# Products of B and the inputs for two of eight state groups moved from VectorE to GpSimd in a state-space layer

## The reference

```python
x_and_res = x @ W_in                          # 128 -> 2 * 256
xs = silu(conv(xc) + conv_b)                  # 256 inner channels
x_dbl = xs @ W_x                              # dt_r (64), Bm (16), Cm (16)
dt = softplus(dt_r @ W_dt + b_dt)
dA = exp(dt[..., None] * A)                   # (batch, time, 256, 16)
dBx = einsum('bld,bln->bldn', dt, Bm) * xs[..., None]
h[t] = dA[t] * h[t - 1] + dBx[t]              # the scan over time
y[t] = einsum('bdn,bn->bd', h[t], C[t]) + xs * D
out = (y * silu(res)) @ W_out
```

## Time and profile before

| | |
|---|---|
| median of 3 runs | 2748.03 us (2746.03 to 2750.99) |
| profiled execution, its own time | 2754.61 us |
| its span | 2752.4 us |
| busy share of the span | PE 87%, PEld 61%, DVE 72%, ACT 64%, POOL 54% |
| first scan to the end of the last (L1797) | 864.0 to 1167.0 us |
| first and last scan 0 of a batch | 863.95 and 1134.24 us, seven periods |

### The profile page before, as it was taken

One profiled execution on the slowest core, in us unless ns is written; L12 is line 12 of the kernel. 1 busy time (PEld: TensorE's weight loads), 2 busy tenths in 40 slices (PEclk: granted clock), 3 DMA queues, 4 the chain that ended last, 5 costly groups with the idle time before them and its releaser, 6 DMA issues.

```text
span 2752.4 us, 93948 instructions
## 1 busy us (share of the span) xinstructions
PE 2392.0 (87%) x35312; PEld 1682.1 (61%) x35340; DVE 1982.8 (72%) x3051; ACT 1770.8 (64%) x3674; POOL 1476.6 (54%) x1060
## 2 busy tenths in 40 slices
PE   7999857896475777768999999999999999999995
PEld 4777535665353334336777777777777767777774
DVE  5888644222325888877888888888888888888883
ACT  4666432333225677666877787778877788777883
POOL 2444324213212444546777777677776777777770
PEclk9999978997787999889999999999999999999998
DMA  9100004772231000001112112211211211121111
GB/s 332 44 0 0 13 22 131 224 223 72 62 108 61 1 0 0 0 16 32 31 53 60 32 30 53 50 42 30 61 38 41 58 46 30 30 69 46 30 30 32
DMA packets 143485, 153.91 MB, mean 56 GB/s; under 512 B 12272, under 2 KB 111920, under 8 KB 142256
## 3 DMA queue, kind: packets, MB, share of 16 engines
q1 hardware_dynamic: 139312, 144.53, 19.1%
q0 software_dynamic: 4096, 8.40, 1.0%
HBM read 75.29 MB, written 27.26 MB: 37 GB/s over the span
## 4 chain that ended last, share of the span: by engine, by line
PE 51%; issue 3%; PEld 1%; DVE 1%; ACT 1%; PEldq 0%; DVEq 0%; POOL 0%; POOLq 0%; ACTq 0%
PE ps L2028 12%; PE ps L2039 6%; PE ps L2126 6%; PE ps L2074 6%; PE ps L2096 5%; PE ps L2152 4%; PE ps L2063 4%; PE ps L2085 3%; PE ps L2161 3%; PE ps L2055 1%; PE ps L2141 1%; PE ps L2134 1%; ACT Y L1406 0%; DVE ss L2531 0%; PEld ps L2126 0%
## 5 line engine op out<-in xcount | busy, mean ns | idle before, releaser
L2427 POOL TENSOR_TENSOR c<-a,bq 128x1024 f32<-128x1024 f32 x192 | 454.0, 2365 | 239.9 <-DVE bq L2524 239.1
L2437 POOL TENSOR_TENSOR qn<-c,ss 128x1024 f32<-128x1024 f32 x192 | 378.0, 1969 | 28.4 <-issue 4.0
L2028 PE MATMUL ps<-wqk,xs 128*128 128x512 f32 x768 | 371.5, 607 | 11.0 <-POOL xs L2420 9.1
L2523 DVE TENSOR_TENSOR a<-ps,tab 128x512 f32<-128x512 f32 x384 | 262.8, 684 | 10.1 <-ACT sq L2234 4.8
L2524 DVE TENSOR_TENSOR bq<-ps,tab 128x512 f32<-128x512 f32 x384 | 261.1, 680 | 0.0
L2445 POOL TENSOR_TENSOR z<-z,sm 128x1024 f32<-128x1024 f32 x96 | 182.6, 1903 | 142.9 <-DVE sm L2552 142.9
L2234 ACT ACTIVATE sq<-ps 128x512 f32<-128x512 f32 x384 | 215.3, 596 | 59.9 <-PE ps L2028 59.7
L2531 DVE TENSOR_REDUCE ss<-sq 128x16 f32<-128x1024 f32 x192 | 230.5, 1217 | 31.0 <-issue 16.6
L1489 POOL TENSOR_TENSOR hC<-hs,Cs 128x1024 f32<-128x1024 f32 x64 | 150.5, 2356 | 176.9 <-ACT Cs L1641 90.4
L2028 PEld LDWEIGHTS ps<-wqk,xs 128*128 128x128 f32 x768 | 140.1, 193 | 136.1 <-issue 129.8
L2039 PEld LDWEIGHTS ps<-ident,qn 128*128 128x128 f32 x1536 | 175.8, 141 | 67.5 <-issue 47.5
(11 more groups left out here) (316 smaller groups left out, 5381.7 us busy)
## 6 DMA issues: line engine op xcount, KB each, us to landing
Vw<-Vs SPq DMA_DIRECT2D x192, 256.0 KB, 4.2
win_rows<-rows_q SPq DMA_DIRECT2D x24, 256.0 KB
outs_q<-win_out SPq DMA_DIRECT2D x24, 256.0 KB
wqk<-in_wqkv SPq DMA_DIRECT2D x6, 1024.0 KB, 5.0
leaves<-in_f_w SPq DMA_DIRECT2D x9, 576.0 KB
leaves<-in_q_w SPq DMA_DIRECT2D x1, 4608.0 KB, 18.8
leaves<-in_k_w SPq DMA_DIRECT2D x1, 4608.0 KB, 22.8
leaves<-in_v_w SPq DMA_DIRECT2D x8, 576.0 KB
```

The source lines that it names most:

```text
L2028: nc.tensor.matmul(jobs.out(n), xs[:, t * 128:(t + 1) * 128], wqk[:, (2 * y + s) * 512:(2 * y + s + 1) * 512], start=True, stop=True).then ...
L2427: nc.gpsimd.tensor_tensor(f(c), f(a), f(bq), ALU.add).then_inc(c_ready.sem, 1)
L2437: nc.gpsimd.tensor_tensor(qn[:, t, y, :, :, :].rearrange("p h s e -> p h (s e)"), c[:, y, :, :, :].rearrange("p h s e -> p h (s e)"), spre ...
L2523: nc.vector.tensor_tensor(a[:, y, :, s, :], Zs, spread(table(0, s), H1), ALU.mult)
```

## The change

For groups 3 and 6 (`SIDE`) the product of B and du is made by GpSimd instead of VectorE. ScalarE copies B of these groups from PSUM to a new SBUF tile `Bs` (`take_B`), and signals it after a drain. GpSimd multiplies it by du into a second new SBUF tile `dBs` in one instruction of 1024 columns. In GpSimd's queue the product for group 3 stands behind read_out 0, the one for group 6 behind read_out 3. In ScalarE's queue take_B 3 stands between decay 1 and decay 2, take_B 6 ahead of decay 6. The scans of groups 3 and 6 read dBs from SBUF in place of dBx in PSUM, and wait for it. GpSimd's loop is written as pairs of batches, since du has two halves.

```diff
--- before.py
+++ after.py
@@ -1424,6 +1424,8 @@
         xdbl = sb("xdbl", [DTR, T])
         dA, hs, hC = (sb(n, [128, 2, 2, 2, T]) for n in ("dA", "hs", "hC"))
         Cs = sb("Cs", [128, 2, 2 * T])
+        SIDE = {3: 0, 6: 1}
+        Bs, dBs = sb("Bs", [128, len(SIDE), 2 * T]), sb("dBs", [128, len(SIDE), 2, 2 * T])
 
         dBx = core.banks.ps[:, 0:2, :]
         S = lambda n, per, credit=0: Count(core.sem("l1a_" + n), per, credit)
@@ -1432,6 +1434,7 @@
             S(n, 1) for n in ("xdbl", "part1", "rest1", "part2", "rest2", "parts", "soft", "dt"))
         dA_ready, hs_ready, hC_ready, hC_used, yy_ready = (
             S("dA", NG), S("hs", NG, 2), S("hC", NG, 2), S("hC_used", NG - 1), S("yy", 1))
+        du_ready, Bs_ready, dB_ready = S("du", 1), S("Bs", len(SIDE)), S("dB", len(SIDE), len(SIDE))
         consts = core.sem("l1a_consts")
         FRONT, MID = range(2)
         order = ((FRONT, "mean", 2), (MID, "Y", 7), (MID, "C2", 3), (MID, "C3", 2), (FRONT, "var", 5), (MID, "C4", 4), (MID, "B4", 6),
@@ -1472,6 +1475,17 @@
                 pool.drain()
                 pool.sem_inc(consts, 1)
                 pool.sem_inc(hC_ready.sem, hC_ready.credit)
+                pool.sem_inc(dB_ready.sem, dB_ready.credit)
+
+                def input_states(b, g, du):
+
+                    i = SIDE[g]
+                    if not (type(b) is int and b == 0):
+                        pool.wait_ge(hs_ready.sem, hs_ready.at(b, g + 1, NG))
+                    pool.wait_ge(du_ready.sem, du_ready.at(b, 1))
+                    pool.wait_ge(Bs_ready.sem, Bs_ready.at(b, i + 1))
+                    nc.gpsimd.tensor_tensor(dBs[:, i, :, :].rearrange("p k (j l) -> p k j l", j=2),
+                                            spread(halves(Bs[:, i, :]), 2), spread(du[:, :, :], 2, 2), ALU.mult).then_inc(dB_ready.sem, 1)
 
                 def read_out(b, g):
 
@@ -1488,11 +1502,17 @@
                     pool.wait_ge(hs_ready.sem, hs_ready.at(b, g + 1))
                     nc.gpsimd.tensor_tensor(four(hC), four(hs), spread(Cs[:, s, :], 2), ALU.mult).then_inc(hC_ready.sem, 1)
 
-                for g in range(NG):
-                    read_out(0, g)
-                with pool.Fori(1, NB) as b:
+                def batch(b, y):
                     for g in range(NG):
                         read_out(b, g)
+                        if g in (0, 3):
+                            input_states(b, g + 3, du2[:, y, :, :])
+
+                batch(0, 0)
+                with pool.Fori(0, (NB - 2) // 2) as pair:
+                    batch(pair * 2 + 1, 1)
+                    batch(pair * 2 + 2, 0)
+                batch(NB - 1, 1)
 
             @block.tensor
             def _(pe):
@@ -1640,6 +1660,13 @@
                     act.wait_ge(*jobs.filled(made(b, f"C{g}"), f"C{g}"))
                     nc.scalar.activation(Cs[:, g % 2, :], jobs.out(f"C{g}"), ACT.Copy).then_inc(jobs.sem_drained(f"C{g}"), 1)
 
+                def take_B(b, g):
+                    act.wait_ge(dB_ready.sem, dB_ready.at(b, SIDE[g] + 1, len(SIDE)))
+                    act.wait_ge(*jobs.filled(made(b, f"B{g}"), f"B{g}"))
+                    nc.scalar.activation(Bs[:, SIDE[g], :], jobs.out(f"B{g}"), ACT.Copy).then_inc(jobs.sem_drained(f"B{g}"), 1)
+                    act.drain()
+                    act.sem_inc(Bs_ready.sem, 1)
+
                 def square_centered(it):
                     act.wait_ge(*jobs.taken(it, "mean"))
                     nc.scalar.activation(lsq[:, :], cent[:, :], ACT.Square).then_inc(squared.sem, 1)
@@ -1698,6 +1725,7 @@
                     new, old = dt2[:, y, :, :], dt2[:, 1 - y, :, :]
                     if mid:
                         decay(b, 1, old)
+                        take_B(b, 3)
                         decay(b, 2, old)
                         take_C(b, 0)
                         decay(b, 3, old)
@@ -1719,6 +1747,7 @@
                         gates(it, xs, sres)
                         take_dbl(it, parts)
                     if mid:
+                        take_B(b, 6)
                         decay(b, 6, old)
                         take_C(b, 5)
                     if front:
@@ -1780,7 +1809,7 @@
 
                 def steps_by_input(dt, du, xs):
                     dve.drain()
-                    nc.vector.tensor_tensor(flat(du), flat(dt), flat(xs), ALU.mult)
+                    nc.vector.tensor_tensor(flat(du), flat(dt), flat(xs), ALU.mult).then_inc(du_ready.sem, 1)
 
                 def input_states(b, g, du):
                     dve.drain()
@@ -1793,8 +1822,12 @@
                     dve.drain()
                     dve.wait_ge(hC_ready.sem, hC_ready.at(b, g + 1, 2))
                     dve.wait_ge(dA_ready.sem, dA_ready.at(b, g + 1))
+                    states = flat(dBx)
+                    if g in SIDE:
+                        states = flat(dBs[:, SIDE[g], :, :])
+                        dve.wait_ge(dB_ready.sem, dB_ready.at(b, SIDE[g] + 1))
                     one_row = lambda t: t[:, g % 2, :, :, :].rearrange("p k j l -> p (k j l)")
-                    nc.vector.tensor_tensor_scan(one_row(hs), one_row(dA), flat(dBx), 0.0, ALU.mult, ALU.add).then_inc(hs_ready.sem, 1)
+                    nc.vector.tensor_tensor_scan(one_row(hs), one_row(dA), states, 0.0, ALU.mult, ALU.add).then_inc(hs_ready.sem, 1)
 
                 def gated(it, xs, sres):
                     dve.wait_ge(*jobs.filled(it, "Y"))
@@ -1820,7 +1853,6 @@
                         center(it)
                     if mid:
                         scan(b, 2)
-                        input_states(b, 3, old_du)
                     if front:
                         by_root(it)
                     if mid:
@@ -1831,8 +1863,6 @@
                         scan(b, 5)
                     if front:
                         first_rest(it, parts)
-                    if mid:
-                        input_states(b, 6, old_du)
                     if front:
                         second_rest(it, parts)
                     if mid:
```

## The result

| | median us | runs |
|---|---|---|
| before | 2749.51 (2745.44 to 2754.06) | 6 |
| changed | 2796.38 (2791.18 to 2805.01) | 6 |

The ratio is 1.0181, with a 95% interval from 1.0165 to 1.0198: the change makes the kernel 46.9 us slower. The forecast was 2804 us with a range from 2781 to 2818.

What follows compares the result with a forecast made beforehand. VectorE was taken to set the stage's pace, with little room in a ring of waits through hC. Seven periods at 7.5 us plus 3 for the last batch gave 55.5 us, hence 2804 us on the median of 2748.0; range 2781 to 2818.

Steps and rivals of the forecast that it cites:

- The main step: State-space stage: removing 2.9 us per batch from VectorE makes it slower through queue waits and blocked scans; slower 0.95.
- Scan 1 to 2: Copy of B 3 on ScalarE makes C 0 1.1 us late, so OUT and add_out wait: VectorE 0.5 us late.
- Scan 2 to 3: dBs 3 ahead of hC 1 delays the copies of C, root_variance and by_root before scan 3: 1.8 us more.
- The blocked scans: Scans 3 and 6, both inputs in SBUF, stand still until GpSimd's hC 2 or hC 5 ends: 0.7 and 2.0 us.
- du held by hC 6: Behind scan 6, hC 6 starts with the product dt and then holds up du: 0.4 us.
- Scan 5 to 6: Copy of B 6 and dBs 6 delay hC 4, which scan 6 needs: 7.3 us where it was 5.02, 2.3 more.
- The sum: Terms give 7.7 us per period, settling at 7.4, taken as 7.5; 55.5 us in all with the last batch.
- scan 0 to 1: Up to the next scan 1 the order is as before and TensorE's Y keeps its distance: nothing.
- The last batch: No front part; hC 1 late by 0.5, scan 4 held by hC 2, scan 6 delayed and held: about 3 us.
- Without blocking: Rival, 14%: queue delay only, scans not stopped by GpSimd; 4.7 us per period, 35 in all, 2783 us.
- Faster: Rival, 3%: both dBs lie in GpSimd's idle time, so VectorE loses 2.9 us per batch: 2725 us.
- the dearer case: Rival, 8%: GpSimd product costs 2.75 us or more, or scans also hold hC: 12 us more, 2816 us.

Runs made afterwards that it cites:

- The run with the pairs kept: Changed kernel, with VectorE still making the removed pairs of products on dBx, where nobody reads them: 2800.06 us, 54.1 more than before.
- the last two runs: Two single edits of the changed kernel: copy of B 3 behind that of C 0, 2778.24 us; dBs 3 ahead of hC 0 on GpSimd, 2791.04 us.
- the scan from SBUF alone: Kernel before, with VectorE writing the products of groups 3 and 6 to SBUF, from where scans 3 and 6 read them: 2761.29 us.
- the run with the copies: Changed kernel with group 6 alone moved, and ScalarE copying the finished dBs to dBx in PSUM for scan 6: 2761.47 us, 14.4 more than before.
- the run with both products moved: Changed kernel, both GpSimd products moved to idle places of its queue, copies of B and making of B 6 reordered: 2763.91 us, 16.8 more than before.

## Why the prediction was right, point by point

**The main step held.** VectorE is the busiest engine of the stage, work was taken from it, and the stage got slower, since each new instruction stands in an in-order queue ahead of one that VectorE waits for, and since two scans were blocked. The run with the pairs kept shows that the saved time lies in waits. The terms below are against the mean of the seven periods before, if nothing else is said.

**Scan 1 to 2** was put at 0.5 us and is 1.9. The place and the order were right: the copy of B 3 at 992.35, C 0 at 994.74, OUT at 995.37, add_out at 997.42. What was mis-sized is TensorE on that path. It had waited 3.29 us for hC 7 before 988.23. The windows around it (PE busy in the third column, PEclk third from the end):

```profile
982.00:986.00 4.00, 2.86 (x8) 0.88 (x6) 3.50 (x2) 0.76 (x2) 0.84 (x2) 1.00 0.00 0
986.00:988.00 2.00, 0.00 (x0) 0.00 (x0) 1.73 (x3) 0.00 (x0) 2.00 (x1) 1.00 0.00 0
988.00:991.30 3.30, 3.07 (x5) 1.09 (x6) 3.14 (x3) 2.18 (x5) 0.17 (x1) 0.62 0.00 0
991.30:995.00 3.70, 1.02 (x5) 0.40 (x3) 3.19 (x5) 2.46 (x6) 0.00 (x0) 0.87 0.00 0
995.00:998.00 3.00, 2.63 (x8) 1.87 (x9) 1.16 (x2) 2.02 (x5) 2.52 (x2) 0.61 0.00 0
```

Right behind the idle stretch the granted clock is 0.62 on average, at half (1.2 GHz) for most of the window and at full (2.4 GHz) for the rest, and in OUT's window 0.61. The four matmuls of over_states 7 take 3.24 us, C 0 with B 3 1.06 and OUT 1.84, where C 0 with B 3 took 0.60 and OUT 1.13. The prediction took these durations at the clock of before. 0.5 for B 3 and 0.7 for OUT make 1.2 of the missing 1.4 us. It is so in every batch: the seven OUT that add_out waited for took 1.84 to 2.08 us at a clock of 0.50 to 0.57, while before five of seven took 1.13 at 1.00. With group 3 alone, two periods had OUT at 1.00 and in 1.13 us, and there scan 1 to 2 took 5.39 and 5.25 us, 0.7 more than the same periods before (4.67 and 4.53); its other periods took 6.3 to 6.8.

**Scan 2 to 3** was put at 1.8 and is 0.7. With scan 2 already late, less of the delay of hC 1 is left to wait for; the sum of both terms was put at 2.3 and is 2.6. That the sum came out near is in part luck. The prediction gave too much of it to dBs 3 and too little to C 0, as the last two runs show.

**The blocked scans.** 0.7 for scan 3 and 2.0 for scan 6 were worked out from one collision of du with hC. Measured are 2.98 - 2.29 = 0.69 and 4.34 - 2.29 = 2.05. The end of the blocked scan is 2.15 us behind the end of the GpSimd product; 2.14 was forecast. Two runs show the cause: the scan from SBUF alone brings 15.4 us, and one PSUM input takes 13.2 away again. du held by hC 6 was put at 0.4 and takes 1.21 to 1.39 us in place of 0.69. Together, scan 6 to 7 is 2.4 us longer than in six of the seven periods before, as forecast, and 2.0 above their mean, for the first of them had a collision of its own (8.36 us). The rule of the Trainium skill (SBUF — State Buffer, Who interferes with whom), that a VectorE instruction with two SBUF inputs contends with a GpSimd instruction that reads SBUF, holds for the scan too; the traces agree (scan 6 beside hC 5: 2.29 us with one input in PSUM in the run with the copies, 4.43 with both in SBUF in the run with group 6 alone).

**Scan 5 to 6** was put at 2.3 and is 1.7 against the mean of before. Scan 6 waits for hC 4 behind dBs 6, as said. The length was forecast at 7.3 us and is 7.03; against the batch shown in the rows the term is 2.0.

**The sum.** The period was forecast at 45 us and is 45.14. The total was 8.6 us too high (55.5 against 46.9). Per period 7.5 us were forecast and 6.5 are measured, 1.9 + 0.7 + 0.7 + 1.7 + 2.0 + 0.1 - 0.6 by the stretches. Most of this difference is the last multiplication: 7.5 us were counted against the period of rows 1, 37.86 us, one of the shortest, while the mean of the seven before is 38.61. The long ones of before held waits for Y and a blocked du, which the new waits swallow. 7 x 0.75 = 5.3 us come from this.

That the period itself came out so near is in part luck. Against the batch of the rows, scan 1 to 2 is 1.3 us above its term, scan 2 to 3 is 0.8 below and scan 5 to 6 0.3 below, and scan 0 to 1 was put at nothing ("TensorE's Y keeps its distance") and is 0.7 shorter: yy comes later and finds Y ready, with 1.3 us of waits in the whole stage where it had 10.3.

In all the seven periods are 7 x (7.5 - 6.53) = 6.8 us too high. The last batch was put at 3 us and is 3.9 longer, which gives 0.9 back; that makes the 5.9 us between the forecast and the stage's 49.6. The last 3 us between the stage and the median stay open: medians stand there against single profiled executions, and these differ as much where no edit was made. The stage begins at 863.95 us before and between 851 and 857 in the changed kernel and all the experiments, and what follows it takes 1585.4 us before and 1590.5 in the changed kernel.

**The rivals.** Without blocking was put at 2783; the blocking is shown. Faster would have needed room of 3.46 us behind hC 1, and it was not there. The price of the GpSimd product, 2.353 us, is that of hC, so the dearer case did not arise from it; that of GpSimd being held did occur: hC 6 by dt in the changed kernel (2.72 us in place of 2.35), at little cost, and hC 5 by scan 6 in the run with both products moved (3.55 us), where dt behind it was held in turn.

## What to carry to other kernels

Taking work off the busiest engine gains nothing where the taker's queue holds instructions that the busiest engine waits for: look up, for the place in the queue and not for the busy share, how late the instruction behind it may be. A VectorE instruction that gets its second input from SBUF in place of PSUM loses its independence of GpSimd; count as its price the rest of whatever GpSimd product will be running then. Price a per-period loss against the mean period, not against a good one, and ask which old waits the new ones will swallow.

## What the runs showed of the hardware

- A blocked VectorE instruction with two SBUF inputs ends a fixed time behind GpSimd's: 2.15 us for the scan of 1024 columns (2.29 alone), 0.55 us for a product of 512 (0.69 alone). It is so to 0.01 us in every such case of all runs.
- It works both ways. When the scan was first, GpSimd's product was held, 3.55 us in place of 2.35, and ended 2.15 us behind the scan. The VectorE product issued as that scan ended did not get in ahead of it: it waited for GpSimd's to end, 2.69 us in place of 0.69.
- GpSimd's product with both inputs repeated costs 2.353 us for 1024 columns, as much as with one repeated.
- Collisions are not alike from batch to batch in an unchanged loop: with group 3 alone moved, three periods had two collisions and were 3 to 4 us longer than the other four. Which kind a period was went with the granted TensorE clock in the 6 us ahead of scan 6: 0.73 to 0.77 in the three, 1.00 in the four, though neither of the colliding engines is TensorE. It hands hC back to GpSimd, and so sets when GpSimd's product starts.
